# Attention values of a pair of heads: one burst on TensorE in place of two, with two places for half of the transposed probabilities

## The reference

```python
scores = jnp.einsum('bhqd,bhkd->bhqk', Q, K_rep) / scale
scores = scores + polarity_bias[None] + (1.0 - gtp[None]) * NEG
attn = jax.nn.softmax(scores, axis=-1)
out = jnp.einsum('bhqk,bhkd->bhqd', attn, V_rep)
```

## Time and profile before

| what | value |
| --- | --- |
| median of 3 runs | 4389.04 us (4388.15 to 4399.78) |
| span of the profiled execution | 4385.1 us |
| TensorE matmul busy | 3923.2 us, 89% of the span |
| VectorE busy | 3009.0 us, 69% |
| ScalarE busy | 2583.3 us, 59% |
| GpSimd busy | 2416.3 us, 55% |
| layer 0, first to last burst of `values_g` | 178.3 to 2838.3 us of the span |

### The profile page before, as it was taken

How to read it: one execution, slowest core, us unless ns; L and a number is a source line. 1 busy time by engine, 2 the same in 40 slices (tenths; PEclk the granted TensorE clock), 3 DMA queues, 4 the chain that set the end, 5 groups by cost and what they waited for, 6 DMA issues and landing times. The chain is left out here.

```text
span 4385.1 us, 105712 instructions
## 1 busy us (share of the span) xinstructions
PE 3923.2 (89%) x37596; PEld 2574.9 (59%) x37596; DVE 3009.0 (69%) x8821; ACT 2583.3 (59%) x6209; POOL 2416.3 (55%) x3854
## 2 busy tenths in 40 slices
PE   3999999999999999999999999829599999999999
PEld 1565555555556655555555566526366666666666
DVE  4676676676666766766666766562387877788786
ACT  2656556556566565565565665502277777777776
POOL 3657566566475565665664755525455545555452
PEclk7999999999999999999999999959799999999999
DMA  4323334233243233342432432123332433324231
GB/s 126 75 77 84 75 76 92 66 95 85 62 99 73 78 82 77 78 93 65 96 79 68 97 75 77 49 94 60 54 64 45 61 58 54 59 49 70 45 54 26
DMA packets 168566, 317.06 MB, mean 72 GB/s; under 512 B 21680, under 2 KB 112112, under 8 KB 162928
## 3 DMA queue, kind: packets, MB, share of 16 engines
q1 hardware_dynamic: 162928, 300.88, 32.0%
q0 software_dynamic: 3968, 5.25, 0.7%
q10 hardware_dynamic: 1152, 4.19, 0.3%
HBM read 126.66 MB, written 32.59 MB: 36 GB/s over the span
## 5 line engine op out<-in xcount | busy, mean ns | idle before, releaser
L1420 POOL TENSOR_SCALAR l_prob_wo<-l_prob_wo,l_recip_g 128x384 f32<-128x384 f32 (+3 forms) x768 | 927.1, 1219 | 259.5 <-DVE l_recip_g L980 257.6
L1871 DVE TENSOR_REDUCE l_neg_max<-l_bank 128x1 f32<-128x512 f32 x1024 | 680.3, 684 | 260.5 <-PE l_bank L1710 259.9
L1997 ACT ACTIVATE l_pts<-l_bank 128x512 f32<-128x512 f32 x1024 | 593.3, 597 | 296.8 <-PE l_bank L1725 288.1
L1248 ACT ACTIVATE l_prob_wo<-l_prob_wo,l_neg_max_g 128x128 f32<-128x128 f32 (+3 forms) x1024 | 571.0, 559 | 297.9 <-DVE l_neg_max_g L974 291.4
L961 DVE CUSTOM_DVE_ANT_0 l_bank<-l_bank,l_mask 128x128 f32<-128x128 f32 (+3 forms) x1024 | 501.0, 500 | 319.8 <-PE l_bank L648 311.9
L974 DVE CUSTOM_DVE_ANT_0 l_prob_wo<-l_bank,l_bias 128x128 f32<-128x128 f32 (+3 forms) x1024 | 476.1, 483 | 342.5 <-PE l_bank L699 319.6
L1240 ACT ACTIVATE l_pts<-l_bank 128x128 f32<-128x128 f32 (+3 forms) x1024 | 439.3, 437 | 443.2 <-PE l_bank L666 426.8
L710 PE MATMUL l_bank<-ident,l_prob_wo 128*128 128x128 f32 x2560 | 426.5, 283 | 84.0 <-POOL l_prob_wo L1420 38.1
L710 PEld LDWEIGHTS l_bank<-ident,l_prob_wo 128*128 128x128 f32 x2560 | 289.1, 141 | 317.0 <-issue 178.6
L1710 PE MATMUL l_bank<-next_ks,l_qs 96*128 96x512 bf16 x1024 | 393.5, 385 | 46.2 <-DVE l_neg_max L1871 23.1
L1725 PEld LDWEIGHTS l_bank<-l_qs,next_ks 128*128 128x128 bf16 x4096 | 303.5, 97 | 181.1 <-ACT l_pts L1997 30.6
(11 more groups left out here) (262 smaller groups left out, 8081.2 us busy)
## 6 DMA issues: line engine op xcount, KB each, us to landing
l_bias<-bias SPq DMA_DIRECT2D x128, 512.0 KB, 4.4
l_qs<-l_parts SPq DMA_DIRECT2D x192, 128.0 KB
l_qs<-l_qs SPq DMA_DIRECT2D x96, 256.0 KB
l_x<-in_x SPq DMA_DIRECT2D x32, 512.0 KB, 4.7
l_kT<-l_bias SPq DMA_DIRECT2D x128, 128.0 KB, 3.2
l_qT<-l_arena SPq DMA_DIRECT2D x128, 128.0 KB, 3.0
l_qT<-l_bias SPq DMA_DIRECT2D x128, 128.0 KB, 3.0
l_prob_wo<-in_Wo SPq DMA_DIRECT2D x16, 1024.0 KB, 4.8
```

The source lines that it names most:

```text
L1248: nc.scalar.activation(prob[qt][:, i, :], prob[qt][:, i, :], ACT.Exp, bias=neg_max_g[:, k:k + 1], scale=-1.0, accum_out=sums_g[:, k:k + 1] ...
L1420: nc.gpsimd.tensor_scalar(prob[qt][:, i, :], prob[qt][:, i, :], recip_g[:, k:k + 1], None, ALU.mult).then_inc(s.g_scaled, 1)
L1871: nc.vector.tensor_reduce(neg_max[:, n % (2 * UNITS):n % (2 * UNITS) + 1], S[n % SB][:, :], AX.X, ALU.max, negate=True).then_inc(s.max_rea ...
L1997: nc.scalar.activation(pts[:, q % 2, u % H, :, :], TB[u % 2][:, :].rearrange("p (j q) -> p j q", j=NT), ACT.Exp, scale=DS ** -0.5).then_in ...
```

## The change

`values_g` loses its argument `k`: one call does both halves, 12 matmuls in a row, at the steps with `r % 8 == 7`. Its signal `g_pv` counts pairs now instead of half pairs, and all waits on it are rewritten to the new count. In `pts_g` the blocks for k = 0 use 2 of 4 places; `turned_at` now puts them into places 0 and 1 for even pairs and 2 and 3 for odd ones. With it, `copy_g` of blocks 0 and 1 of pair g waits for the burst of pair g-2, and of blocks 2 and 3 for that of pair g-1.

```diff
+        def turned_at(g, k):
+            return 2 * (g % 2) if k == 0 else 0
...
-                def values_g(b, g, k):
-                    done = BEATS * b + 4 * g + 2 * k + 2
+                def values_g(b, g):
+                    done = BEATS * b + 4 * g + 4
                     pe.wait_ge(s.g_copied_v, done)
                     pe.wait_ge(s.g_copied_a, done)
-                    if k == 0:
-                        wait(pe, s.g_out, PAIRS * b + g)
...
-                    last = 2 * k + 1
-                    for j in range(last + 1):
...
+                    for k in range(2):
+                        last = 2 * k + 1
+                        for j in range(last + 1):
+                            skip = P if j == last else 0
+                            for i in range(2):
+                                m = nc.tensor.matmul(OT[64 * i:64 * (i + 1), 2 * P * k + skip:2 * P * (k + 1)], v0[:, j, g // 2, :],
+                                                     pts_g[:, k, i, turned_at(g, k) + j, skip:2 * P], start=j == 0, stop=j == last)
                     m.then_inc(s.g_pv, 1)
...
-                        if r >= 75 and r % 8 in (3, 7):
-                            values_g(f, (r - 75) // 8, (r - 75) // 4 % 2)
+                        if r >= 79 and r % 8 == 7:
+                            values_g(f, (r - 79) // 8)
...
-                        if r in (3, 7):
-                            values_g(f - 1, 7, (r - 3) // 4)
+                        if r == 7:
+                            values_g(f - 1, 7)
...
                 def copy_g(b, p):
                     g, qt = divmod(p, NT)
                     dve.wait_ge(s.g_turned, UNITS * b + 2 * p + 1)
-                    wait(dve, s.g_pv, 2 * PAIRS * b + 2 * g + qt // 2 - 1)
+                    wait(dve, s.g_pv, PAIRS * b + g - 1 + qt // 2)
...
                 def copy_out_g(b, g):
-                    act.wait_ge(s.g_pv, 2 * PAIRS * b + 2 * g + 2)
+                    act.wait_ge(s.g_pv, PAIRS * b + g + 1)
```

More of the change, by code:

```diff
@@ L711, in turn_g @@
                     m.then_inc(s.g_turned, 1)
-                def values_g(b, g, k):
-                    done = BEATS * b + 4 * g + 2 * k + 2
+                def values_g(b, g):
+                    done = BEATS * b + 4 * g + 4
                     pe.wait_ge(s.g_copied_v, done)
                     pe.wait_ge(s.g_copied_a, done)
-                    if k == 0:
-                        wait(pe, s.g_out, PAIRS * b + g)
[L719 to L722, removed]
-                    last = 2 * k + 1
-                    for j in range(last + 1):
[L725 to L728, removed]
+                    wait(pe, s.g_out, PAIRS * b + g)
+                    if g == 0:
+                        pe.wait_ge(s.out_turned, 4 * (b + 1))
+                        for half in range(2):
+                            pe.wait_ge(*W.emptied(("v0", b, half)))
+                    for k in range(2):
[5 more added lines that the diff above has]
+                                                     pts_g[:, k, i, turned_at(g, k) + j, skip:2 * P], start=j == 0, stop=j == last)
                     m.then_inc(s.g_pv, 1)
@@ L992, in copy_g @@
                     off = qt % 2 * P
-                    nc.vector.tensor_copy(pts_g[:, qt // 2, 0, 0:qt + 1, off:off + P],
+                    at = turned_at(g, qt // 2)
+                    nc.vector.tensor_copy(pts_g[:, qt // 2, 0, at:at + qt + 1, off:off + P],
                                           PT[0][:, 0:(qt + 1) * P].rearrange("p (j q) -> p j q", q=P)).then_inc(s.g_copied_v, 1)
@@ L1238, in exponentials @@
                     if u % UNITS == 0:
-                        wait(act, s.g_pv, 2 * PAIRS * b)
+                        wait(act, s.g_pv, PAIRS * b)
                     nc.scalar.activation(pts[:, q % 2, i, 0:w, :], TB[u % 2][:, 0:w * P].rearrange("p (j q) -> p j q", j=w),
@@ L1253, in copy_g @@
                     act.wait_ge(s.g_turned, UNITS * b + 2 * p + 2)
-                    wait(act, s.g_pv, 2 * PAIRS * b + 2 * g + qt // 2 - 1)
+                    wait(act, s.g_pv, PAIRS * b + g - 1 + qt // 2)
                     if g == 0:
@@ L1257, in copy_g @@
                     off = qt % 2 * P
-                    nc.scalar.copy(pts_g[:, qt // 2, 1, 0:qt + 1, off:off + P],
+                    at = turned_at(g, qt // 2)
+                    nc.scalar.copy(pts_g[:, qt // 2, 1, at:at + qt + 1, off:off + P],
                                    PT[1][:, 0:(qt + 1) * P].rearrange("p (j q) -> p j q", q=P)).then_inc(s.g_copied_a, 1)
                 def copy_out_g(b, g):
-                    act.wait_ge(s.g_pv, 2 * PAIRS * b + 2 * g + 2)
+                    act.wait_ge(s.g_pv, PAIRS * b + g + 1)
                     if b > 0:
```

## The result

The changed kernel takes 4405.68 us (median of 16 runs, 4396.37 to 4419.74), the kernel before 4395.52 (16 runs): a ratio of 1.0026, 95% interval 1.0018 to 1.0034. So it is 10 us slower, where 9 us faster was forecast. The profiled execution has a span of 4395.5 us against 4385.1, and all of the 10.4 us lies in layer 0: the end of its last burst comes 10.36 us later.

What follows compares the result with a forecast made beforehand. TensorE's own work, with some waits, was taken to bound the grouped half. Of 22 us saved in switches, grown waits left 9 through the `kT` DMA: 4389.0 to 4380, range 4364 to 4398 (8 in 10).

Steps and rivals of the forecast that it cites:

- Pair 1: Second pair of the grouped half: no wait, so TensorE's shift goes to -0.25 us, then +0.40 behind the longer burst.
- What bounds the kernel now: Grouped half: TensorE's own work with some waits, busy 89.05 of 96 us, granted clock 1.00 (2.4 GHz).
- the walk: One image followed pair by pair with TensorE's shift: -0.60 us at its end, time 4380, chance 0.48.
- What the change takes away: Array shape switches at the short burst: TensorE gains 0.90 or 0.75 us there; net 1.4 an image, 22 in all.
- What costs nothing: Later products for two blocks add no wait; the second place in `pts_g` spares VectorE a hold-up to the burst's 2.3 us.
- Pair 0: First pair: the 0.75 us gained is lost in a wait for VectorE's copy, growing from 0.63 to about 1.3; then +0.65.
- Pairs 2, 3, 4, 6: TensorE's shift from one long burst's end to the next: 0.00, -0.10, 0.00 and -0.25 us an image.
- The DMA of `kT`: Start of the next image: it arrives 0.60 us earlier, TensorE's 0.63 wait nearly vanishes; 9 us over 15 passages.
- The sum: Whole kernel: TensorE's shift of -0.60 us an image, 9 us off the median 4389.0, giving 4380.
- the third: Rival: the short burst was free between waits, and the longer one pushes scores back 0.65 us; slower, 4403, chance 0.13.
- the first: Rival: waits do not grow, as VectorE and GpSimd have spare time and slide forward; 22 us off, 4367, chance 0.22.
- the second: Rival: nothing shows, cover lost equals switches saved and `kT`'s DMA is held by something else; 4389, chance 0.17.

Runs made afterwards that it cites:

- e2: Changed kernel with the change undone for pair 5 alone (its short burst back at the old place): 4390.88 us, ratio 0.9993 to the kernel before.
- e5: Changed kernel with one block's two score products issued twice, ahead of the wait at pair 5: 4403.33 us, ratio 1.0016 to the kernel before.
- e14: Changed kernel without the second place in `pts_g` for the first two query blocks: 4415.94 us, ratio 1.0053 to the kernel before.
- e9: Changed kernel with two projection matmuls ahead of pair 1 issued earlier, two score products (pair 5) and five transpositions (pair 2) issued twice: 4379.09 us, ratio 0.9966.
- e13: Kernel before with the same three edits as e9 (projection matmuls earlier, score products and five transpositions issued twice): 4391.59 us, ratio 0.9994.
- e8: Changed kernel with SyncE's load of the next image's `x` issued ahead of the last pair's bias: 4372.47 us, ratio 0.9943 to the kernel before.
- e11: Kernel before with the load of the next image's `x` issued ahead of the last pair's bias: 4358.89 us, ratio 0.9923.
- e4: Changed kernel with two projection fill matmuls ahead of pair 1 issued at step 77 in place of 80 and 81: 4398.75 us, ratio 1.0008.

## Why the prediction was wrong

The step that failed first is "Pair 1: no wait in it; -0.25, then +0.40". TensorE's timeline shows none there, and so I took the fill behind the short burst for work that can come earlier. But the rope's last row ends within 0.1 us of the fill's start: a wait of almost nothing is a wait that the work ahead has just covered. What the runs showed in its place is a wait for the bank of some 0.80 us in every image, 12.4 us more in all than before. e1, which undoes the change there, takes it away: its list of waits has no such line, and over pair 1 its shift is -0.03 in place of +0.62. Its time can't show the gain, as falls at pair 2 ate it.

The step that failed second is in "What bounds the kernel now": a clock of 1.00 was read once and taken for fixed. At pair 5 the walk had the wait right (1.58, forecast 1.5) and stopped there; behind it the clock falls in 5 of the 14 images that have the wait, 8 us. e2 and e5 remove these falls, e2 with 15 us of time. That work put back ahead of the wait takes the falls away is shown; that the 0.12 us by which the wait grew would make them by itself is not. 12.4 and 8 are 20 us, and forecast and result are 19 apart (9 faster, 10 slower). The rest of the miss in microseconds is the median of before, 4389.0 of the three runs shown and 4395.5 of sixteen.

The other steps, in their order:
- **What the change takes away** held. Where the short burst left, the shift fell by 0.80 to 0.98 us at pairs 0, 2, 3 and 5 (forecast 0.75) and by 0.71 to 1.0 at pairs 4, 6 and 7 (0.90), and the burst of 24 records holds TensorE 2.31 us (from its start to that of the scores behind it), 2.3 forecast. The busy time fell by 15.6; with the 8 us that the slower clock adds it would be 23.6, against 22.
- **What costs nothing** held: the bursts (L730) wait 0.7 us in all, for nothing that another engine does, and e14 shows what the second place is worth, 12 us.
- **Pair 0** held in its sum and not in its form: the single wait of 0.63 did not become 1.3 but 0.77, and two more of 0.30 and 0.28 us stand ahead of it.
- **Pairs 2, 3, 4, 6** were within 0.1 us each, pair 7 within 0.2.
- **The DMA of `kT`** gave back 0.61 where 0.65 was forecast.
- **The sum** of -0.60 an image was not reached in any fair comparison. e9 has -0.64 against the kernel before, but that is luck: it keeps 0.60 us of the wait at pair 1, and its earlier fill wins something in the kernel before too. Against e13 it is -0.33, and most of the gap is again pair 1 (+0.14, forecast -0.25).
- **The rivals**: the third, slower, named the sign and nearly the time (4403), but by another mechanism. It saw no loss at pair 1, and no clock. That the waits don't grow, the first, is refuted by the 21 us at L713; the second, that nothing shows, by the steps above.

## What to carry to other kernels

Ahead of taking work out from between two waits, look at every instruction that follows it for how narrowly its inputs and its bank came in time, not only at those that waited: a slack of 0.1 us under 0.9 us of removed work is a wait of 0.8. When waits on TensorE get longer, read the granted clock behind them image by image, and price a fall (1.6 us here) for each. Judge such a change with the same edits in both kernels, and by the stage that it touches: 10 us slower alone; 2 to 5 us faster in layer 0 of the traces with the same work doubled and moved in both (e9 against e13), where the medians say 12; and about as much slower as at first with the loads better ordered in both (e8 against e11).

## What the runs showed of the hardware

- In the changed kernel the granted clock fell to 0.5 inside the grouped half behind single waits of 1.44 to 1.62 us (pair 5), in e4's image 5 behind two waits of 1.40 us together (pair 2), and only in some images; before, behind waits of 1.28 to 1.61 us at pair 5 with the short burst ahead of them, it fell in none of 14. It stayed low for 3.41 us in most, for up to 13.65 us in e4.
- Doing work twice made the kernel faster: e9 against e4, 1.35 us more work an image, 18 us less time.
- The lower clock at the start of the grouped half (3.41 or 6.83 us in nearly every image) is in every trace: in the first 15 images 71.7 us before, 75.1 in the changed kernel, 61 to 102 in the experiments; nothing was tried on it.
